# Indirect DMAs that wait for the landing of the one three places ahead, in an adaLN and mixture-of-experts kernel

## What is computed

```
x = x + L0_ffn(L0_cond(x))                   # 8 experts, all rows, gated by a threshold
xn = layernorm(L1_cond(x)) * gamma + beta
probs = softmax(xn @ gate_w)
w, idx = top_k(probs, 2);  w = w / sum(w)
h = gelu(xn @ w1[e] + b1[e]);  out_e = h @ w2[e] + b2[e]
x = x + sum over the two chosen e of w * out_e  + residual of L1
```

## Time and profile before

| what | us |
|---|---|
| median of three runs | 396.54 (393.29 to 401.63) |
| the profiled execution | 395.97 |
| its span, first to last instruction | 394.1 |
| TensorE busy | 338.7 (86%) |
| VectorE busy | 282.7 (72%) |
| ScalarE busy | 250.0 (63%) |
| GpSimd busy | 101.9 (26%) |
| L1634, 32 indirect DMAs, median of one | 0.958 |
| L1816, 43 indirect DMAs, median of one | 0.958 |

### The profile page before, as it was taken

One profiled execution on the slowest core, in us unless ns is written; L12 is line 12 of the kernel. 1 busy time (PEld: TensorE's weight loads), 2 busy tenths in 40 slices (PEclk: granted clock), 3 DMA queues, 4 the chain that ended last, 5 costly groups with the idle time before them and its releaser, 6 DMA issues.

```text
span 394.1 us, 9605 instructions
## 1 busy us (share of the span) xinstructions
PE 338.7 (86%) x3422; PEld 243.9 (62%) x3422; DVE 282.7 (72%) x779; ACT 250.0 (63%) x345; POOL 101.9 (26%) x97
## 2 busy tenths in 40 slices
PE   8999999888999999999979969699886934889930
PEld 5657776666777666767756646477664713567720
DVE  1746589999999978798977999735666422546684
ACT  3368588677998887998887758455653503346520
POOL 0000000000000000122227575404345372526770
PEclk9897999999999999999999989799986885999995
DMA  6993003022443674500001012211211012121354
GB/s 189 291 373 107 2 0 98 25 70 58 124 151 130 228 245 173 220 2 2 2 0 42 16 49 59 71 23 41 63 27 55 16 54 69 39 57 55 116 148 141
DMA packets 27059, 35.80 MB, mean 91 GB/s; under 512 B 6581, under 2 KB 22853, under 8 KB 26789
## 3 DMA queue, kind: packets, MB, share of 16 engines
q1 hardware_dynamic: 21600, 28.40, 23.1%
q0 software_dynamic: 2400, 4.95, 3.8%
q10 hardware_dynamic: 3012, 1.84, 1.5%
HBM read 29.18 MB, written 16.25 MB: 115 GB/s over the span
## 4 chain that ended last, share of the span: by engine, by line
PE 61%; DVE 16%; issue 8%; ACT 6%; another core or an unknown queue 5%; DMA 2%; POOL 1%; ACTq 0%; DVEq 0%; SPq 0%; POOLq 0%
PE bank L663 5%; DVE l L710 5%; PE psA L616 5%; PE psA L617 5%; PE psA L618 5%; PE bank L665 5%; PE bank L664 5%; PE bank L653 4%; PE psA L601 4%; PE psA L597 3%; PE psA L603 3%; PE psA L602 2%; PE bank L654 2%; PE bank L1068 2%
## 5 line engine op out<-in xcount | busy, mean ns | idle before, releaser
L710 DVE SCALAR_TENSOR_TENSOR l<-h 128x1024 f16<-128x1024 f32 (+1 forms) x90 | 104.7, 1165 | 15.3 <-ACT h L703 15.0
L663 PE MATMUL bank<-w,h 128*128 128x128 f16 x512 | 91.2, 221 | 3.4 <-issue 2.1
L689 ACT ACTIVATE h<-psA,b1f 128x512 f32<-128x512 f32 (+1 forms) x100 | 76.7, 800 | 25.6 <-PE psA L618 21.9
L703 ACT ACTIVATE h<-h 128x1024 f16<-128x1024 f32 (+1 forms) x90 | 91.0, 1011 | 1.4
L665 PE MATMUL bank<-w,l 128*128 128x128 f16 x512 | 91.2, 221 | 0.0
L664 PE MATMUL bank<-w,h 128*128 128x128 f16 x512 | 91.1, 221 | 0.0
L1816 POOL DMA_INDIRECT sorted_out<-w,xe x43 | 50.3, 1169 | 49.0 <-DVE w L1865 23.3
L684 ACT ACTIVATE h<-psA 128x1024 f32<-128x1024 f32 (+1 forms) x22 | 22.1, 1004 | 59.9 <-PE psA L603 42.6
L663 PEld LDWEIGHTS bank<-w,h 128*128 128x128 f16 x512 | 50.5, 99 | 13.9 <-issue 6.0
L1404 POOL TENSOR_SCALAR rs<-mv 128x4 f32<-128x4 f32 x8 | 4.0, 498 | 200.3 <-DVE mv L1385 199.9
L664 PEld LDWEIGHTS bank<-w,h 128*128 128x128 f16 x512 | 50.5, 99 | 5.6
(11 more groups left out here) (214 smaller groups left out, 574.3 us busy)
## 6 DMA issues: line engine op xcount, KB each, us to landing
sorted_in<-in_pad SPq DMA_DIRECT2D x14, 715.0 KB, 7.1
w<-in_w SPq DMA_DIRECT2D x8, 512.0 KB, 5.6
wraw<-in_w SPq DMA_DIRECT2D x8, 512.0 KB, 3.8
first<-sorted_in SPq DMA_DIRECT2D x43, 65.0 KB
w<-sorted_out SPq DMA_DIRECT2D x6, 256.0 KB, 3.9
mg<-in_maskt SPq DMA_DIRECT2D x8, 128.5 KB, 3.5
acc<-in_xtm SPq DMA_DIRECT2D x2, 512.0 KB, 5.5
mg<-in_gbc SPq DMA_DIRECT2D x8, 128.0 KB
```

What stands on the lines that cost most here:

```text
L663: pe.matmul(oo, a, w_h, start=(c == 0 and k == 0), stop=False, skip_group_check=True)
L689: last = act.activation(dst[:, q * w:q * w + w], src[:, q * w:q * w + w], ACT.Gelu_apprx_tanh, bias=b1f[:, es[q] * 4 + c:es[q] * 4 + c + 1 ...
L703: act.activation(wide(h16, h16_at[u], u), wide(h32, h32_at[u], u), ACT.Copy, scale=HS).then_inc(s_hi, 1)
L710: dve.scalar_tensor_tensor(wide(l16, h16_at[u], u), wide(h32, h32_at[u], u), HS, wide(h16, h16_at[u], u), ALU.mult, ALU.subtract).then_inc ...
```

## The change

Every indirect DMA of the two kinds now waits until the DMA of its kind three places ahead of it has landed. The 32 scatters share three semaphores in turn (n modulo 3, counted over all groups) instead of one for each group, and whoever waited for a whole group now waits for all three semaphores. The order of the instructions is the same on every engine. 29 scatters and 40 L1816 DMAs get a wait more; from i = 8 an L1816 DMA has four waits where it had three.

```diff
+LAG = 3
-        t_sc = [sem(f"t_sc{g}") for g in range(NG)]
+        t_sc = [sem(f"t_sc{s}") for s in range(LAG)]
+        def sorted_in(eng, g):
+
+            for s in range(LAG):
+                eng.wait_ge(t_sc[s], 16 * len([n for n in range(8 * g + 8) if n % LAG == s]))
             def rows_free(eng):
                 if g >= 2:
-                    eng.wait_ge(t_sc[g - 2], 16 * 8)
+                    sorted_in(eng, g - 2)
+                    n = 8 * g + 4 * k + i
+                    if n >= LAG:
+                        pool.wait_ge(t_sc[n % LAG], 16 * (n // LAG))
                     pool.indirect_dma_start(scx, bass.IndirectOffsetOnAxis(idx[:, g, k, i:i + 1], 0),
-                                            xsf[:, 4 * (g % 2) + i, :], None).then_inc(t_sc[g], 16)
+                                            xsf[:, 4 * (g % 2) + i, :], None).then_inc(t_sc[n % LAG], 16)
                     for g in BATCH[b]:
-                        sp.wait_ge(t_sc[g], 16 * 8)
+                        sorted_in(sp, g)
                 if i >= NSO:
                     pool.wait_ge(t_so[i % NSO], 16 * (i // NSO))
+                if i >= LAG:
+                    pool.wait_ge(t_so[(i - LAG) % NSO], 16 * ((i - LAG) // NSO + 1))
```

## The result

The changed kernel takes 395.28 us (median of 20 runs, 391.73 to 403.8), the kernel before 395.47 us (20 runs, 388.11 to 401.63). The ratio is 1.0066 with a 95% interval of 1.0038 to 1.0095. The two medians are almost equal and the ratio isn't 1, because runs more than 1.5% above a kernel's fastest are left out of the ratio, and the kernel before had one run of 388.11, which leaves only its six quickest runs in. From this comparison alone I would not trust the 0.7%; the means of all 20 runs, 395.5 and 395.1 us, differ by 0.1%. So I take it that the new waits cost 0.6 to 0.7%, about 2.5 us; that the whole kernel became slower by as much is not shown by this series alone. I had forecast 396.5 us and no change, with 0.3 us of loss counted in.

What follows compares the result with a forecast made beforehand. It took TensorE and the two engines behind it to bound the kernel. 395.97 + 0 + 0.3 = 396.3 us, or 396.8 from the runs' median, gave a forecast of 396.5 us, range 381 to 400.5.

Steps and rivals of the forecast that it cites:

- What bounds the kernel: Whole kernel: TensorE, with 61% of the chain, and the two engines behind it; GpSimd holds 1%.
- The 69 waits, 2.40 us needed and 2.82 there: GpSimd's new waits: each is over 0.42 us before it would cost anything; cost 0, upper bound 3.0 us.
- in every row of DMAs: GpSimd's waits: the 0.42 us to spare holds in all rows, however long the DMA ahead takes.
- For the last L1816 DMAs I count no cover: End of the kernel: nothing was counted as hiding a delay of the last L1816 DMAs.
- for a late landing or two: Term of 0.3 us for the new waits on SyncE, VectorE and ScalarE, also standing for late landings.
- Landings are late under load: Rival, chance 0.06: DMAs three ahead land 1.8 us later, five waits end 1.38 us late, 403.2 us at most.
- The stalls go away: Rival, chance 0.33: stalls in rows of indirect DMAs come from queued DMAs and vanish, 17.4 us, giving 378.9 us.
- My doubt: Against the stalls going away: no path seen from GpSimd's queue to TensorE's semaphores; group 1's row has no stall.
- Each wait costs a fresh start: Rival, chance 0.08: each waiting indirect DMA on GpSimd costs 1.01 us more, together 14.1, giving 410.4 us.
- The waits of the others: New waits on SyncE (five), VectorE (eight), ScalarE (four): at most 0.7 us, taken as 0.3.
- no effect: Whole kernel: no stall less and no wait that costs, chance 0.53; within 2%, chance 0.64.

Runs made afterwards that it cites:

- 61 waits of 69: The changed kernel, but the last eight L1816 DMAs don't wait for the one three in front; ratio to the kernel before 0.9987.
- quarter loads: The changed kernel with SyncE's six result loads cut from 256 KB to 64 KB each; ratio to the kernel before 0.9999.
- a distance of one: The changed kernel with each indirect DMA waiting for the one just in front; 453.47 us, ratio 1.2115; again in a series with stalls, 457.88 us beside 396.17.
- a distance of two on the scatters: The changed kernel with scatters waiting for the one two ahead and L1816 DMAs for none; 0.9906, and 1.0107 in a series without stalls.
- the tile waits alone: The kernel before with only the L1816 DMAs' waits added, each for the one three places in front; ratio 1.0066.
- one wait in: The kernel before with a single wait added, L1816 DMA number 39 waiting until number 36 has landed; ratio 1.0061.
- one wait out: The changed kernel with the single wait of L1816 DMA number 39 taken out; median 396.9 us in 6 runs against 396.18 for the kernel before.
- one of two: The changed kernel with scatters and L1816 DMAs each waiting for the one two places ahead; ratio 0.9796, again 0.9887.

## Why the prediction was wrong

**What bounds the kernel:** right. TensorE's share of the chain is 60% against 61%, and nothing changed before the first indirect DMA.

**The 69 waits, 2.40 us needed and 2.82 there:** right in most rows of DMAs, and right about the cost away from the end. The kernel with the 29 waits of the scatters measured 1.0005, that with 61 waits of 69 0.9987. One at a time the need was mostly smaller than my bound, 1.58 us for a scatter and 2.11 for a tile DMA. Wrong was "in every row of DMAs": in the kernel with 61 waits four of them came late, with gaps of up to 1.9 us, and in the changed kernel the fifth scatter, on which group 1's normalisation step depends, starts 0.57 us after the fourth instead of 0.30. That these cost nothing is what the times say, not my sum.

**"For the last L1816 DMAs I count no cover", and then 0.3 us "for a late landing or two":** this is the step that failed. The absence of cover was right and the lateness was not. I took the time to a landing, 1.39 us after the end of the DMA at the latest, from the last DMA of all, a place where nothing else moves, and used it for places at which SyncE's six loads move 1.5 MB. There it is 7.05 - 1.68 = 5.37 us after its end. Even the quiet place gives no upper bound: the last DMA of the changed kernel lands 2.58 - 0.96 = 1.62 us after its end. My term of 0.3 us should have been 2.15 us, once, by the row after; the kernels with that wait measured 0.6 to 0.7%, some 2.5 us. The loads stand in the kernel before too, from 370.22 us on, and its timeline of SyncE would have told me to look.

**Landings are late under load (0.06):** this is the case that came about, with two things wrong in it. I looked for the load at group 1's scatters, whose DMA share of 0.12 spoke against it, and priced groups 0 and 1 with four of five late landings. Late landings came in several places, and the only one that cost time that can be measured came at the end, where the kernel reads its own results. The Trainium skill's rule on HBM access under load, 0.2 us on average and 2 us at high load, pointed the right way ("DMA: Bandwidth & Descriptors", section Latency and other measured facts). The trace shows more than its figure: from its end this DMA takes 5.37 us to land and the last one 1.62, so the landing is 3.75 us later, with six loads of 256 KB under way.

**The stalls go away (0.33):** not at a distance of three; 19.4 us before, 12.1 in the chain after, and ScalarE's longest wait 10.2 in place of 14.6 could be taken for a start, but the changed kernel with quarter loads has all its waits at three, too, and this row:

```profile
ACT h L690 <- remote: 14.8, 1, 14.8
```

My doubt was that I saw no path from GpSimd's queue to TensorE's semaphores. I still don't know one, but the link is shown: in a series with stalls a distance of one leaves none of ScalarE's remote waits behind the first indirect DMA (one profile), and a distance of two on the scatters removes the stalls before 270 us (four profiles). The forecast had the right suspicion with the wrong dose. Its argument that no remote wait stands ahead of the first indirect DMA holds for its own trace, not for all: four later profiles have one of 1.7 to 3.5 us at about 21 us. The page's instruction queues bring nothing between 312 and 333 us in the kernel before, so no load of instructions was under way in the large stall. What stays open is whether it needs fewer DMAs out or only a slower row, why group 1's row is free of stalls, and what the series without stalls have that the others lack: the kernels that were to tell these apart met no stalls.

**Each wait costs a fresh start (0.08):** refuted. In the changed kernel the scatters in a row start 0.30 us after the one ahead, all but one, and the kernel with their waits is level.

**The waits of the others:** a small slip. SyncE gets eight waits more, not five (four become twelve), so the bound is 20 x 0.043 = 0.9 us and not 0.7. No run shows a cost.

**The chances:** the time, 395.28, lies where I said, and the difference of 0.7% is within the 2% that I called no change. The claim itself was "no effect", and it has one that can be measured.

## To carry to other kernels

A wait on something that happened long ago cost nothing that could be measured here; so look for the one place where it didn't happen long ago, and read the time to a landing there and not at a quiet spot. Here that place was where another queue starts large loads, and at the end of the kernel nothing covered it. Where a chain names a wait without a cause, compare several series before a forecast rests on it: here 20 us of stalls came and went with the series.

## What the runs showed of the hardware

Landing of an indirect DMA of 128 rows: most often 2.2 to 2.6 us from its start in the chains here, 4.1 to 7.05 us while six loads of 256 KB, issued within 3.4 us on SyncE's queue, are under way (7.05 in the changed kernel, 5.99, 5.78 and 5.17 in the kernels with the tile waits alone, one wait in and one wait out, 4.2 with a distance of one, 4.1 with one of two). With loads of 64 KB there was no gap left in the tail. Single landings of 3 to 4.6 us come elsewhere too, for a reason that no run here was made to find.

From the end of an indirect DMA to the start of one that waits for its landing, one at a time: mostly 1.58 us for scatters and 2.11 us for tile DMAs, with two scatters out up to 2.2 us. The one that starts mostly has its plain 0.96 us, not the 1.69 us of the earlier trace rows. So 1.69 us comes with another reason than with having waited, one that no run here shows.

In some series of runs, and not in others, engines stand still for 3 to 15 us during rows of indirect DMAs, most of which start 1.26 us apart, with nothing in the profile that they wait for. The time of the same kernel was 374 us without and 394 to 396 us with that. A kernel that waits for each landing before the next DMA had none of it in its one profile from such a series, and took 16% longer there and 21% longer in a series without stalls.
